# One attention stage of a fused four-layer kernel: biases moved from VectorE into matmuls, value copy moved to ScalarE, transposes of the next row moved to the end of a window

## What is computed

```python
q = rms_norm(x @ Wq + bq, gq)                  # rows of 256, 16 heads of 16
k_img = rms_norm(ctx @ Wk_img + bk_img, gk_img)
v_img = ctx @ Wv_img + bv_img
out = softmax(q k_img^T / 4) v_img @ Wo + bo   # added to x
x = x + out;  x = x + feed_forward(layernorm(x))   # 4-bit fake quantisation
```

## Time and profile before

| what | value |
|---|---|
| median of 3 runs | 1291.06 us (1290.24 to 1292.5) |
| the profiled execution's own time | 1285.59 us |
| its span, first to last instruction | 1283.8 us |
| granted TensorE clock over the span | 0.955 of 2.4 GHz |
| PE busy | 1088.0 us, 85% of the span |
| DVE, ACT, POOL busy | 704.6, 506.5, 320.5 us (55%, 39%, 25%) |

### The profile page before, as it was taken

One profiled execution on the slowest core, in us unless ns is written; L12 is line 12 of the kernel. 1 busy time (PEld: TensorE's weight loads), 2 busy tenths in 40 slices (PEclk: granted clock), 3 DMA queues, 4 the chain that ended last, 5 costly groups with the idle time before them and its releaser, 6 DMA issues.

```text
span 1283.8 us, 20548 instructions
## 1 busy us (share of the span) xinstructions
PE 1088.0 (85%) x7122; PEld 824.0 (64%) x7138; DVE 704.6 (55%) x1700; ACT 506.5 (39%) x1787; POOL 320.5 (25%) x440
## 2 busy tenths in 40 slices
PE   1788886899997788799999999996888999985684
PEld 0355443899996466588888888884555556553463
DVE  5877745212223788854555445555656666664334
ACT  0255562232321466643334333333445555542121
POOL 5544210222322355420000000002122222210562
PEclk9999997899998699999999999998989999998797
DMA  6443305898883070000000000140000000000785
GB/s 191 120 134 108 99 15 178 308 333 317 326 328 114 1 263 2 1 28 20 1 2 1 1 1 1 33 132 1 1 1 9 5 5 5 6 5 9 238 254 183
DMA packets 59731, 121.31 MB, mean 94 GB/s; under 512 B 9049, under 2 KB 37481, under 8 KB 53713
## 3 DMA queue, kind: packets, MB, share of 16 engines
q1 hardware_dynamic: 52169, 106.61, 24.8%
q0 software_dynamic: 4416, 12.06, 2.9%
q10 hardware_dynamic: 3044, 1.33, 0.4%
HBM read 107.29 MB, written 12.49 MB: 93 GB/s over the span
## 4 chain that ended last, share of the span: by engine, by line
PE 62%; DVE 17%; issue 7%; ACT 6%; DMA 4%; POOL 2%; SPq 1%; ACTq 0%; DVEq 0%; POOLq 0%
PE P L819 6%; PE P L829 6%; PE P L1742 4%; PE P L1735 4%; PE P L1787 4%; PE P L1751 4%; ACT big L2139 3%; DVE small L440 2%; PE P L2659 2%; PE P L1880 2%; PE P L1760 2%; PE P L1775 2%; PE P L1886 2%; PE P L288 2%; PE P L316 2%
## 5 line engine op out<-in xcount | busy, mean ns | idle before, releaser
L139 POOL TENSOR_TENSOR lrs<-lve,mhalf 128x1 f32<-128x1 f32 x64 | 36.7, 574 | 363.5 <-DVE lve L130 332.0
L440 DVE TENSOR_REDUCE small<-P 128x2 f32<-128x512 f32 x128 | 83.4, 682 | 38.6 <-PE P L288 37.9
L2050 ACT ACTIVATE big<-P,small 128x128 f32<-128x128 f32 x128 | 45.4, 367 | 145.0 <-DVE small L2228 145.0
L859 ACT ACTIVATE big<-P,big 128x128 f32<-128x128 f32 x184 | 52.6, 369 | 123.2 <-PE P L819 101.6
L510 ACT ACTIVATE big<-P 128x512 f32<-128x512 f32 x128 | 72.4, 598 | 60.4 <-PE P L301 55.3
L819 PE MATMUL P<-big 128*128 128x128 f32 x736 | 88.0, 279 | 0.4 <-DMA big<-b_w 0.2
L819 PEld LDWEIGHTS P<-big 128*128 128x128 f32 x736 | 85.8, 195 | 1.2 <-issue 0.6
L829 PE MATMUL P<-big 128*128 128x256 f32 x368 | 83.1, 379 | 0.0
L288 PE MATMUL P<-big 90*128 90x256 bf16 x256 | 55.6, 307 | 31.8 <-DMA big<-scr_qk 17.2
L2219 DVE COPY big<-P 128x512 f32<-128x512 f32 x32 | 22.1, 692 | 107.0 <-PE P L1751 107.0
L952 DVE COPY big<-P 128x256 f32<-128x256 f32 x23 | 9.8, 425 | 125.4 <-PE P L829 125.4
(11 more groups left out here) (380 smaller groups left out, 2578.5 us busy)
## 6 DMA issues: line engine op xcount, KB each, us to landing
big<-b_w SPq DMA_DIRECT2D x23, 1028.0 KB
big<-b_w SPq DMA_DIRECT2D x23, 1024.0 KB
big<-scr_qk SPq DMA_DIRECT2D x96, 96.0 KB
big<-i_wgu SPq DMA_DIRECT2D x23, 352.0 KB
big<-moe_y SPq DMA_DIRECT2D x16, 256.0 KB, 4.1
big<-i_wd SPq DMA_DIRECT2D x23, 176.0 KB
scr_qk<-big SPq DMA_DIRECT2D x8, 384.0 KB
moe_x<-XN SPq DMA_DIRECT2D x16, 128.0 KB, 1.7
```

Of the source, the lines that this page charges most:

```text
L440: dve.tensor_reduce(negM[:, h, :], P[:, h % 2, :].rearrange("p (c s) -> p c s", c=2), AX.X, ALU.max, negate=True).then_inc(a_max, 1)
```

## The change

Query and key biases enter PSUM as the first matmul of each accumulation: the row `ones[0:1, :]` as the stationary operand and the bias row `cbqk` as the moving one, one of 256 columns for the keys at the head of `project_context`, one for the queries at the head of `project_rows`. `bias` and `values` are gone from DVE, and `c_qk` with them; ACT copies the values into `c_vp` (two strided `Copy`) at the head of `squares_values`, then squares straight from PSUM, and `normalise` reads PSUM too. The value bias is multiplied by the output weight once, before the windows (2 matmuls of 256 columns, then one sum on DVE into `cbo`), which is right because the weights of a softmax add up to one. `turn` moves to behind `weigh` in the odd windows of rows -1 to 5, and on DVE `normalise` moves to behind `divide` and `copy_probs`. `scores(0)` and the first residual bias on POOL get a wait for the folded bias. Two loads shrink (the bias row is no longer spread over 128 partitions, the value bias comes as 128 by 2).

```diff
--- before.py
+++ after.py
@@ -1031,7 +1031,7 @@
 
         ar2, ar3 = Arena(big2), Arena(big3)
         ar3.at = 2304
-        c_qk, c_qn, c_junk = (ar2.view([128, 2, D]) for _ in range(3))
+        c_qn, c_junk = (ar2.view([128, 2, D]) for _ in range(2))
         c_qT = [ar2.view([128, 4, T]) for _ in range(2)]
         c_kb = [ar2.view([128, KD, 4, T]) for _ in range(2)]
         c_vp = [ar2.view([128, H, 32]) for _ in range(3)]
@@ -1044,8 +1044,8 @@
         d_tmp = ar2.view([128, D])
         cw = ar3.view([128, KD, 3 * D])
         cwo = ar3.view([128, KD, D])
-        cbqk, cgqk = ar3.view([128, 2 * D]), ar3.view([128, 2 * D])
-        cbv, cbo = ar3.view([128, D]), ar3.view([128, D])
+        cbqk, cgqk = ar3.view([1, 2 * D]), ar3.view([128, 2 * D])
+        cbv, cbo = ar3.view([128, KD]), ar3.view([128, D])
         hm = sm.view([128, 4])
         after = Arena(big3)
         after.at = ar3.at
@@ -1086,8 +1086,8 @@
         def s2_sp(sp):
             sp.wait_ge(xn_ready, 2 * B)
             for dst, src in ((cw, c_w.rearrange("(k p) n -> p k n", p=128)),
-                             (cwo, c_wo.rearrange("(k p) n -> p k n", p=128)), (cbqk, rows(c_bqk)),
-                             (cgqk, rows(c_gqk)), (cbv, rows(c_bv)), (cbo, rows(c_bo)), (hm, head16)):
+                             (cwo, c_wo.rearrange("(k p) n -> p k n", p=128)), (cbqk, c_bqk),
+                             (cgqk, rows(c_gqk)), (cbv, c_bv), (cbo, rows(c_bo)), (hm, head16)):
                 sp.dma_start(dst, src).then_inc(c_ld, 16)
             for dst, src in ((d_w1f, d_w1.rearrange("(k p) f -> p k f", p=128)),
                              (d_w2f, d_w2.rearrange("(f p) d -> p f d", p=128)), (d_b1c, d_b1), (d_b2b, rows(d_b2)),
@@ -1176,15 +1176,17 @@
                     pe.wait_ge(c_v, n)
                 if n >= 4:
                     pe.wait_ge(tb_ev, TURNED[n - 3])
+                pe.matmul(P[:, QK_BANK[n], D:2 * D], ones[0:1, :], cbqk[:, D:2 * D], start=True, stop=False)
                 for w, dst in ((1, P[:, QK_BANK[n], D:2 * D]), (2, P[:, V_BANK[n], 0:D])):
                     for k in range(KD):
-                        pe.matmul(dst, CT[:, k, n * T:n * T + T], cw[:, k, w * D:w * D + D], start=(k == 0),
+                        pe.matmul(dst, CT[:, k, n * T:n * T + T], cw[:, k, w * D:w * D + D], start=(w == 2 and k == 0),
                                   stop=(k == KD - 1))
 
             def project_rows(n):
+                pe.matmul(P[:, QK_BANK[n], 0:D], ones[0:1, :], cbqk[:, 0:D], start=True, stop=False)
                 pe.wait_ge(tb_ev, B + n + 1)
                 for k in range(KD):
-                    t = pe.matmul(P[:, QK_BANK[n], 0:D], XNT[:, k, n * T:n * T + T], cw[:, k, 0:D], start=(k == 0),
+                    t = pe.matmul(P[:, QK_BANK[n], 0:D], XNT[:, k, n * T:n * T + T], cw[:, k, 0:D], start=False,
                                   stop=(k == KD - 1))
                 t.then_inc(c_pj, 1)
 
@@ -1206,6 +1208,8 @@
                 n, c = divmod(h, 2)
                 pe.wait_ge(c_qkT, n + 1)
                 pe.wait_ge(c_kbd, h + 1)
+                if h == 0:
+                    pe.wait_ge(c_qkf, 2)
                 if h == 1:
                     pe.wait_ge(c_qkT, 2)
                     pe.wait_ge(c_v, 2)
@@ -1284,6 +1288,10 @@
                 t.then_inc(d_dn, 1)
 
             pe.wait_ge(c_ld, 112)
+            for k in range(KD):
+                t = pe.matmul(P[:, 2, 0:D], cbv[:, k:k + 1].broadcast_to([128, 128]), cwo[:, k, :], start=(k == 0),
+                              stop=(k == KD - 1))
+            t.then_inc(c_qkf, 1)
             project_context(0)
             project_context(1)
             turn_routed(0)
@@ -1306,14 +1314,15 @@
                 else:
                     if 0 <= k - 1 < B:
                         turn_rows(k, 1)
-                    if 0 <= k + 2 < B:
-                        turn(k + 2)
                     if k == -2:
+                        turn(0)
                         project_rows(1)
                 if 0 <= k - 2 < B:
                     up(k - 2, odd)
                 if 0 <= w < HALVES:
                     weigh(w)
+                if odd and 1 <= k + 2 < B:
+                    turn(k + 2)
                 if 1 <= w + 5 < B:
                     turn_routed(w + 5)
             return output, turn_rows, up, down
@@ -1335,14 +1344,23 @@
                                        ACT.Exp, bias=c_m[h % 2][:, j:j + 1])
                 t.then_inc(c_exp, 1)
 
-            def squares(n):
-                act.wait_ge(c_qkf, n + 1)
+            def squares_values(n):
+                act.wait_ge(c_pj, n + 1)
                 if n > 0:
                     act.wait_ge(c_ss, n)
                 if n >= 2:
                     act.wait_ge(c_ve, n - 1)
+                pair = lambda v: v.rearrange("p (q i d) -> p q i d", i=2, d=16)
+                if n >= 3:
+                    act.wait_ge(c_pv, 2 * n - 4)
+                if n == 0:
+                    act.wait_ge(c_cb, 1)
+                for i in range(2):
+                    t = act.activation(c_vp[n % 3].rearrange("p (q i) d -> p q i d", i=2)[:, :, i, 16 * i:16 * i + 16],
+                                       pair(P[:, V_BANK[n], 0:D])[:, :, i, :], ACT.Copy)
+                t.then_inc(c_v, 1)
                 for a in range(2):
-                    t = act.activation(c_junk[:, a, :], c_qk[:, a, :], ACT.Square, accum_out=c_sst[:, n % 2, a:a + 1])
+                    t = act.activation(c_junk[:, a, :], P[:, QK_BANK[n], a * D:a * D + D], ACT.Square, accum_out=c_sst[:, n % 2, a:a + 1])
                 t.then_inc(c_ss, 1)
 
             def copy_qk(n):
@@ -1384,7 +1402,7 @@
                     exps(w + 1)
                 if not odd:
                     if 0 <= k + 2 < B:
-                        squares(k + 2)
+                        squares_values(k + 2)
                 else:
                     if 0 <= k - 1 < B:
                         copy_rows(k, 1)
@@ -1397,29 +1415,12 @@
             return copy_rows, relu
 
         def s23_dve(dve):
-            def bias(n):
-                dve.wait_ge(c_pj, n + 1)
-                if n > 0:
-                    dve.wait_ge(c_ss, n)
-                    dve.wait_ge(c_qkn, n)
-                dve.tensor_tensor(c_qk.rearrange("p a d -> p (a d)"), P[:, QK_BANK[n], :], cbqk, ALU.add).then_inc(c_qkf, 1)
-
-            def values(n):
-                if n >= 3:
-                    dve.wait_ge(c_pv, 2 * n - 4)
-                for i in range(2):
-                    pair = lambda v: v.rearrange("p (q i d) -> p q i d", i=2, d=16)[:, :, i, :]
-                    t = dve.tensor_tensor(c_vp[n % 3].rearrange("p (q i) d -> p q i d", i=2)[:, :, i, 16 * i:16 * i + 16],
-                                          pair(P[:, V_BANK[n], 0:D]), pair(cbv), ALU.add)
-                t.then_inc(c_v, 1)
-
             def normalise(n):
                 dve.wait_ge(c_rs, n + 1)
-                dve.wait_ge(c_qkf, n + 1)
                 if n > 0:
                     dve.wait_ge(c_tr, n)
                 for a in range(2):
-                    t = dve.scalar_tensor_tensor(out=c_qn[:, a, :], in0=c_qk[:, a, :], scalar=c_rst[:, n % 2, a:a + 1],
+                    t = dve.scalar_tensor_tensor(out=c_qn[:, a, :], in0=P[:, QK_BANK[n], a * D:a * D + D], scalar=c_rst[:, n % 2, a:a + 1],
                                                  in1=cgqk[:, a * D:a * D + D], op0=ALU.mult, op1=ALU.mult)
                 t.then_inc(c_qkn, 1)
 
@@ -1486,16 +1487,18 @@
             routed_row(dve, 1)
             dve.wait_ge(c_ld, 112)
             dve.wait_ge(c_cb, 1)
+            dve.wait_ge(c_qkf, 1)
+            dve.tensor_tensor(cbo, cbo, P[:, 2, 0:D], ALU.add).then_inc(c_qkf, 1)
             for w in WINDOWS:
                 k, odd = divmod(w, 2)
                 if 0 <= w + 1 < HALVES:
                     maxima(w + 1)
-                if odd and 0 <= k + 2 < B:
-                    normalise(k + 2)
                 if odd and 0 <= w - 1 < HALVES:
                     divide(w - 1)
                 if 0 <= w < HALVES:
                     copy_probs(w)
+                if odd and 0 <= k + 2 < B:
+                    normalise(k + 2)
                 if not odd:
                     if 0 <= k - 1 < B:
                         add(k - 1)
@@ -1505,9 +1508,6 @@
                         apply("attend", k - 1)
                     if 0 <= k - 3 < B:
                         apply("feed", k - 3)
-                    if 0 <= k + 2 < B:
-                        bias(k + 2)
-                        values(k + 2)
                 else:
                     if 0 <= k - 2 < B:
                         quantise(k - 2, 0)
@@ -1581,6 +1581,8 @@
                     if 2 <= w + 6 < B:
                         routed(w + 6)
                 else:
+                    if k == 0:
+                        pool.wait_ge(c_qkf, 2)
                     if 0 <= k < B:
                         bias(k)
```

(2 more changed lines are left out.)

## The result

| | before | changed |
|---|---|---|
| median of 10 runs | 1288.64 us | 1299.18 us |
| range | 1285.63 to 1294.06 | 1293.73 to 1308.26 |
| profiled execution, span | 1283.8 us | 1298.3 us |

Ratio changed to before **1.0078, 95% interval 1.0058 to 1.0099**: slower by about 10 us, clear of the 0.2% a measurement can tell. The forecast was no change (1291.7 us) and the range ended at 1297.0.

The account below looks back on a forecast made before the run. Took the rows to be paced by a loop going back and forth between PE and DVE, neither full. Terms -0.8+0.95+0.4+0.9-0.8 = +0.65 on 1285.6 us profiled, the median 5.5 above: 1291.7 us; range 1285.0 to 1297.0.

Parts of the forecast that it names:

- Bias as one-row matmuls: Query and key biases on PE: two instructions of 256 columns a row, 0.43 us each, 0.87 us a row, all on the path.
- +0.4 before the scores of half 1: Queries' bias of row 1, in the start at half clock: 0 to 0.9 us, as waits may hide it; +0.4 taken.
- rival "slower": About 1296 us: PE's two waits a row bring half clock in three of rows 2 to 5, +4.3 us; chance 0.27.
- +0.9 for the whole row: Row 0: later `maxima`, 1.2 us back from `normalise`, 0.87 more for PE; +0.9 us, between -1 and +1.7.
- walk of the odd window: Times from S, the start of its scores: `weigh` S+4.3, `turn` S+5.3, PE window ends S+5.75, `down` S+9.4; new row 15.3 us.
- new wait of `down`: PE's `down` waits 0.8 us for DVE's second `quantise`, queued behind `turn`, `copy_qk` and `relu`.
- Rows 2 to 5: Three rows of 15.3 us, then 5.0 and 9.4: 60.3 us against 61.1 before, so -0.8 us.
- term of +0.95 for DVE's lateness: Behind rows 2 to 5, to `up` in row 6: 3.5 us from `down` where it was 2.55, so +0.95 us.
- Row 1: No relu or `down` there: 13.2 us with part of a routed turn, against 14.0 before, so -0.8 us.
- The folding: Before the windows: two matmuls (0.87 us) and a DVE sum (0.45), hidden while both engines wait for gathered rows; costs nothing.
- The faster rival: About 1286.5 us: loop over relu looser than walked, bias 0.27, `quantise` unhindered by POOL, start hidden, rows 14.6; chance 0.33.

## Why the prediction was wrong

- **The step that failed: "Bias as one-row matmuls".** The prediction put 0.43 us on each, between bounds of 0.28 and 0.43, and 0.87 on a row. Both bounds were on the cheap side: I let the full-height projection be the upper end because no row of the trace had lower weights that cost more. Measured: 0.62 each, and with what the neighbours lose 1.55 a row, 0.68 more than the 0.87 in the sum. From four rows that is 2.7 us, and it grows at the start, where one such matmul takes 1.15 us from start to start at half clock (439.73 to 440.88). So the +0.4 before the scores of half 1 came out as +1.4: the queries' bias of row 1 takes 1.15 us there (424.59 to 425.74), and no wait hides it.
- **What no term held: the clock at the start.** The rival "slower" looked for half clock in rows 2 to 5, through PE's waits, and found none there: their clock is 1.00. In rows 0 to 5 it fell on a stretch without any wait, the even window of row 0: the forecast had +0.9 for the whole row, the trace has +5.9 for its even window and -2.4 for the odd, +3.5 together. What decided there was the form of the bias matmuls and not a wait.
- **The walk of the odd window was right.** `weigh` at S+4.29 (said 4.3), `turn` at S+5.31 (5.3), the next scores at S+5.90 (5.75). The new wait of `down` was named with its size, 0.8 us, and measures 0.76. `down` starts at S+9.68 (9.4): the second `quantise` took 0.97+0.58 (start to end 1.59) instead of 1.25, longer than the 1.33 of before, and `down` itself takes 0.97 before a one-row matmul instead of 0.87. Row: 15.3 said, 16.35 measured; 0.68 of the 1.05 is the bias, 0.3 `quantise`, 0.1 `down`.
- **Rows 2 to 5** then come to +3.0 instead of -0.8, and the even window of row 6 to +2.6. The term of +0.95 for DVE's lateness was right: `up` starts 3.42 us behind `down` (541.13 less 537.71) where 3.5 was said and 2.55 was before. What no term held is that, behind this wait of 2.38 us, `up` and `weigh` run at half clock, 2.81 us where they took 1.54; there the slower rival's mechanism did come, but outside the rows in which it was looked for. The rest, 0.4, is the new wait of `down` (0.76) less what the `scores` there lost at half clock before (1.57 from start to start in place of 1.06).
- **Row 1** gave +0.1 in place of -0.8. It took 14.47 us where 13.2 was said: 0.78 of that is the bias and its neighbours, the rest are transposes of a routed row (0.37 where 0.1 was put) and a `turn` and `output` of 0.59 and 0.96 for 0.44 and 0.87. **The folding** cost nothing, as said: from L952 to the first transposes of a routed row it is 10.05 us before and 10.04 after.
- **By part**, the forecast is short by 1.0 us before the scores of half 1, 2.6 in row 0, 0.9 in row 1, 3.8 in rows 2 to 5 and 1.6 in row 6: 9.9 of the 10 that are missing.
- The faster rival assumed what turned out dear to be cheap. Its other half, that the late queue on ACT would not bind, fell too; taking `relu` out of it gained 0.4 to 0.5%.

## What to carry to other kernels

Before moving a step late on one engine, list what is queued behind its consumer on every other engine; here `relu` on ACT and `quantise` on POOL were, and reordering those two together with the late turn won 0.6% (0.9936) with the arithmetic untouched, where the late turn alone won nothing (1.0001). A bias folded into an accumulation is an extra matmul on the engine that bounds the loop, at 0.43 us for 256 columns, 0.62 if it has one row of weights; if it must be a matmul, make it full height. And if no row of the trace has the shape that you price, let the range go above the nearest row as well as below it.

## What was not expected of the hardware

A matmul with a single row of weights (1x256, 32-bit) takes 0.62 us from start to start where one with 128 rows takes 0.43, and the instructions around it are slower: the four behind it together by 0.19 us (1.92 against 1.73), the eight bf16 ones ahead by 0.1 (0.97 against 0.87). Whether it is the single row or the change of height that costs was not tried. And where such matmuls stand in a stretch at 1.2 GHz, the granted clock came up late: a mean of 0.53 to 0.62 over that stretch in four kernels with them, 0.68 to 0.79 in twelve without, PE busy by its records in either case. Why it came late stays open. In full-clock rows they did not bring it down: 1.00 in rows 1 to 5 of the changed kernel.

The two records that a 32-bit matmul shows, called two passes ahead of the prediction, do not make it twice as dear as a bf16 one. For 256 columns at full clock it is 0.43 us against 0.11 (eight in 0.87, 508.75 to 509.62 in the kernel before): four times.
